# A drain of VectorE in place of the semaphore wait, where one Sinkhorn chain runs alone

## What is computed

```python
        def sinkhorn_log(logits, num_iters=SINKHORN_ITERS, tau=SINKHORN_TAU):
            Z = logits / tau
            ...
            def step(carry, _):
                u, v = carry
                u = -jax.nn.logsumexp(Z + v[..., None, :], axis=-1)
                v = -jax.nn.logsumexp(Z + u[..., :, None], axis=-2)
                return ((u, v), None)
            (u, v), _ = jax.lax.scan(step, (u0, v0), None, length=num_iters)
            return jnp.exp(Z + u[..., :, None] + v[..., None, :])
        ...
        H_res = sinkhorn_log(H_res_logits)
        H_pre = jax.nn.softmax(H_pre_logits, axis=-1)
        H_post = jax.nn.softmax(H_post_logits, axis=-1)
        g = jax.nn.sigmoid(gate)[0]
        I = jnp.eye(n, dtype=H_res.dtype)
        H_res = (1.0 - g) * I + g * H_res
        ...
        x_pre = jnp.einsum('btnc,btn->btc', x_streams, H_pre)
        y = x_pre @ W_branch
        x_mixed = jnp.einsum('btij,btjc->btic', H_res, x_streams)
        y_distributed = jnp.einsum('btc,btn->btnc', y, H_post)
        return (x_mixed + y_distributed).reshape(B, T, nC)
```

## Time and profile before

| | us |
|---|---|
| median of 3 runs (1103.5 to 1104.36) | 1104.23 |
| the profiled execution's own time | 1103.76 |
| its span | 1102.0 |
| PE busy | 1072.5 (97%) |
| DVE busy | 813.6 (74%) |
| ACT busy | 485.3 (44%) |
| POOL busy | 201.1 (18%) |

### The profile page before, as it was taken

One profiled execution on the slowest core, in us unless ns is written; L12 is line 12 of the kernel. 1 busy time (PEld: TensorE's weight loads), 2 busy tenths in 40 slices (PEclk: granted clock), 3 DMA queues, 4 the chain that ended last, 5 costly groups with the idle time before them and its releaser, 6 DMA issues.

```text
span 1102.0 us, 17847 instructions
## 1 busy us (share of the span) xinstructions
PE 1072.5 (97%) x6394; PEld 900.0 (82%) x6394; DVE 813.6 (74%) x1942; ACT 485.3 (44%) x1040; POOL 201.1 (18%) x199
## 2 busy tenths in 40 slices
PE   7999999999999999999999999999999999999578
PEld 6888888788888888888888888888888878888457
DVE  6887668667667878776667877757546798758998
ACT  4544434444444446544444455434313434342417
POOL 3000000223223233332332321000001032140001
PEclk9999999999999999999999999999999999999899
DMA  9975775255553333245445312699934705000001
GB/s 235 184 197 132 160 161 139 54 110 110 113 101 84 76 77 71 60 92 113 95 110 114 77 34 59 124 214 243 209 68 105 122 21 79 2 15 1 1 1 77
DMA packets 184830, 111.29 MB, mean 101 GB/s; under 512 B 108072, under 2 KB 174504, under 8 KB 184768
## 3 DMA queue, kind: packets, MB, share of 16 engines
q1 hardware_dynamic: 183136, 109.17, 46.2%
q10 hardware_dynamic: 1632, 1.31, 0.4%
HBM read 90.98 MB, written 18.94 MB: 100 GB/s over the span
## 4 chain that ended last, share of the span: by engine, by line
PE 90%; DVE 8%; DMA 1%; ACT 1%; issue 0%; ACTq 0%; DVEq 0%
PE ps L693 32%; PE ps L660 14%; PE ps L534 14%; PE ps L1041 8%; PE ps L523 4%; PE ps L721 4%; PE ps L704 4%; PE ps L1029 2%; PE ps L559 2%; PE ps L804 2%; DMA raw<-in_L_xattn_q_proj_w 1%; DVE small L2234 1%; DVE small L2238 1%; DVE small L2226 1%; DVE small L2230 1%; DVE small L2222 1%
## 5 line engine op out<-in xcount | busy, mean ns | idle before, releaser
L693 PE MATMUL ps<-wt,act 128*128 128x512 f32 x1536 | 381.1, 394 | 0.0
L693 PEld LDWEIGHTS ps<-wt,act 128*128 128x128 f32 x1536 | 278.1, 188 | 51.9 <-issue 0.4
L660 PE MATMUL ps<-act,wt 128*128 128x512 f32 x672 | 153.7, 390 | 0.0
L534 PE MATMUL ps<-wt,act 128*128 128x512 f32 x672 | 153.1, 389 | 0.0
L1171 ACT ACTIVATE wt<-raw 128x512 fp32r<-128x512 f32 x192 | 106.7, 625 | 93.2 <-PE ps L534 51.8
L534 PEld LDWEIGHTS ps<-wt,act 128*128 128x128 f32 x672 | 125.9, 188 | 26.0
L660 PEld LDWEIGHTS ps<-act,wt 128*128 128x128 f32 x672 | 125.8, 188 | 26.0
L1637 DVE STREAM_TRANSPOSE raw<-raw 128x1024 f32<-128x1024 f32 x92 | 107.9, 1217 | 22.1 <-DMA raw<-in_L_xattn_o_proj_w 21.2
L1041 PE MATMUL ps<-wt,act 128*128 128x512 f32 x480 | 121.4, 400 | 0.0
L1645 DVE TENSOR_TENSOR wt<-raw,wt 128x512 fp32r<-128x512 f32 x168 | 105.0, 682 | 16.4 <-ACT wt L1171 16.3
L2472 POOL TENSOR_TENSOR small<-small 128x4 f32<-128x4 f32 (+2 forms) x64 | 69.3, 1085 | 241.6 <-DVE small L1659 197.2
(11 more groups left out here) (188 smaller groups left out, 1324.7 us busy)
## 6 DMA issues: line engine op xcount, KB each, us to landing
xr<-in_ctx SPq DMA_DIRECT2D x64, 256.0 KB, 4.8
raw<-in_L_xattn_o_proj_w SPq DMA_DIRECT2D x32, 512.0 KB, 14.6
raw<-in_L_xattn_q_proj_w SPq DMA_DIRECT2D x28, 512.0 KB, 9.5
xr<-q_rows SPq DMA_DIRECT2D x16, 512.0 KB, 4.2
ot_hi<-spare SPq DMA_DIRECT2D x64, 128.0 KB, 2.0
act<-ot_hi SPq DMA_DIRECT2D x32, 256.0 KB, 10.2
q_rows<-G SPq DMA_DIRECT2D x28, 256.0 KB, 3.0
raw<-in_L_xattn_k_proj_w SPq DMA_DIRECT2D x8, 512.0 KB, 6.5
```

The costliest lines, as they stand in the source:

```text
L534: mm = pe.matmul(banks[t], lhs(p == 2, c, t), wt[:, n_slot, int(p == 1), c, :], start=(acc_from and q == 0), stop=(acc_to and q == 3 * NC ...
L660: mm = pe.matmul(acc[h], wt[:, par, int(p == 1), c, h * P:(h + 1) * P], act[:, 0, int(p == 2), c * UW:(c + 1) * UW], start=(q == 0), stop= ...
L693: mm = pe.matmul(bank, src[int(p == 2)][:, c, kt * P:(kt + 1) * P], wt[:, slot, int(p == 1), c, :], start=(q == 0), stop=(q == 3 * NC - 1))
```

## The change

`iterate` tells its steps when one chain is alone and nothing stands beside it. Then each of the six steps is preceded by `v.drain()`, an instruction of its own that holds VectorE's queue until the engine has finished what was issued, in place of the wait for `sk_step[c]`. The steps raise the semaphore as before. No instruction changes its place on any engine. That holds for five iterations of chain 0 at its beginning and for five of chain 2 at its end: 60 waits go and 60 drains come (VectorE's program has 2007 instructions in place of 1947). Fold steps and all iterations with two chains or with work beside keep the semaphore.

```diff
@@ -2155,6 +2155,12 @@
+            def settled(c, alone):
+                if alone:
+                    v.drain()
+                else:
+                    stepped(c)
+
...
-            def scale_cols(c):
-                stepped(c)
+            def scale_cols(c, alone=False):
+                settled(c, alone)
                 step(c, v.tensor_tensor(rows4(of(tk, c)), rows4(of(Kx, c)), over_i(ub[c]), ALU.mult))
 
-            def sum_rows(c, y):
-                stepped(c)
+            def sum_rows(c, y, alone=False):
+                settled(c, alone)
                 step(c, v.tensor_reduce(ua[c], rows3(of(y, c)), AX, ALU.add))
...
             def iterate(chains, beside=None):
 
+                alone = len(chains) == 1 and beside is None
                 fold = [c for c in chains if iterated[c] == folds[c]]
                 for c in chains:
                     iterated[c] += 1
                     if c in fold:
                         fold_outer(c)
                     else:
-                        scale_cols(c)
+                        scale_cols(c, alone)
...
                 for c in chains:
-                    sum_rows(c, Kx if c in fold else tk)
+                    sum_rows(c, Kx if c in fold else tk, alone)
...
                 for c in chains:
-                    invert_cols(c)
+                    invert_cols(c, alone)
```

More of the change, by code:

```diff
@@ L2214, in centre_cols, with invert_rows, scale_rows, sum_cols @@
                 step(c, v.reciprocal(ua[c], ua[c]))
-            def scale_cols(c):
-                stepped(c)
+            def scale_cols(c, alone=False):
+                settled(c, alone)
                 step(c, v.tensor_tensor(rows4(of(tk, c)), rows4(of(Kx, c)), over_i(ub[c]), ALU.mult))
-            def sum_rows(c, y):
-                stepped(c)
+            def sum_rows(c, y, alone=False):
+                settled(c, alone)
                 step(c, v.tensor_reduce(ua[c], rows3(of(y, c)), AX, ALU.add))
-            def invert_rows(c):
-                stepped(c)
+            def invert_rows(c, alone=False):
+                settled(c, alone)
                 step(c, v.reciprocal(ua[c], ua[c]))
-            def scale_rows(c):
-                stepped(c)
+            def scale_rows(c, alone=False):
+                settled(c, alone)
                 step(c, v.tensor_tensor(rows3(of(tk, c)), rows3(of(Kx, c)), over_j(ua[c]), ALU.mult))
-            def sum_cols(c):
-                stepped(c)
+            def sum_cols(c, alone=False):
+                settled(c, alone)
                 step(c, v.tensor_reduce(two(ub[c]), cols4(of(tk, c)), AX, ALU.add))
-            def invert_cols(c):
-                stepped(c)
+            def invert_cols(c, alone=False):
+                settled(c, alone)
                 step(c, v.reciprocal(ub[c], ub[c]))
@@ L2282, in iterate @@
                 for c in chains:
-                    invert_rows(c)
+                    invert_rows(c, alone)
                 if beside:
@@ L2286, in iterate @@
                 for c in chains:
-                    scale_rows(c)
+                    scale_rows(c, alone)
                 if beside:
@@ L2290, in iterate @@
                 for c in chains:
-                    sum_cols(c)
+                    sum_cols(c, alone)
                 if beside:
```

## The result

| | us |
|---|---|
| before, median of 9 runs (1103.15 to 1105.07) | 1104.09 |
| with the drains, median of 9 runs (1106.31 to 1109.41) | 1107.08 |
| ratio, with its 95% interval | 1.003 [1.0021, 1.0038] |
| the profiled execution's own time, and its span | 1109.41, 1107.6 |

The change makes the kernel 3.0 us slower, by the interval between 2.3 and 4.2. The forecast was 1107.0.

A forecast was written before the change was run, and what follows sets the result against it. PE, busy 97%, was taken as the bound, VectorE's steps mattering only where PE waits. Terms 0.76 + 0.84 + 1.14 = 2.74 us on 1104.23 gave 1107.0 us, range 1103.9 to 1110.0.

The forecast's parts named there:

- The bound and the seams: VectorE's steps matter only where PE waits: chain 0's lone iterations before 1019 us; chain 2's lie beside PE's last 23.62 us.
- x: Change in cost per lone step with a drain: taken as +0.07 us, bounded by -0.035 and +0.115.
- chain 0, first 18 steps: Three lone iterations before 1004.45 us: 1.26 us later, less 0.50 idle at line 2088, leaving 0.76 us.
- chain 0, next 12 steps: 1006.72 to 1009.49 us: 12 x 0.07 = 0.84 us, no idle time behind them, all reaching PE.
- chain 2, 30 steps: Kernel's end, 1087.45 to 1093.78 us: 2.10 us later, less 0.96 slack at the store, leaving 1.14 us.
- the slack is 0.96 us: At the last stores: SyncE's lands near 1100.56, ScalarE's near 1101.52 us, so 0.96 us of chain 2's delay is covered.
- tile 3's *first* diagonal: Ready at 1094.84 us, needed by PE near 1096.5: 1.6 us of slack, 0.5 us late after the change.
- SyncE's store would end the kernel: Sign at the kernel's end: POOL and SyncE's last store end the kernel instead of ScalarE's.
- costs no more than the wait: Rival at the lone steps: x between -0.035 and 0.03, time 1104.1 to 1104.6 us; chance 0.12.
- waits for the empty pipe either way: Rival at every lone step: a flush between operations sets the spacing, x = 0, time stays 1104.2 us; chance 0.10.
- Heavier: Rival at the lone steps: drain handshake makes x 0.09 to 0.15; 1109.7 us at 0.115, 1111.8 at 0.15; chance 0.16.
- The clock: Rival: TensorE's granted clock falls at PE's longer wait; 1.7 us seemed too little for that; chance 0.02.

The follow-up runs named there:

- first_only: Against the kernel before: drains only before chain 0's 30 lone steps, chain 2's keep the semaphore; 1106.34 us against 1103.74, ratio 1.0023.
- last_only: Against the kernel before: drains only before chain 2's 30 lone steps; 1104.88 us against 1103.74, ratio 1.0015.
- own_wait: Against the changed kernel: each drain replaced by a separate wait for the same semaphore, the step keeping its own; 1107.23 us against 1103.74 before, ratio 1.0034.
- two_drains: Against the changed kernel: two drains in place of one before each of the 60 lone steps; 1112.16 us against 1103.74 before, ratio 1.0083.
- late_attached: Kernel before, line 2260's last-ending wait put inside the step, the other ahead; doubled wait before chains 1 and 2's loop removed; 1103.55 us against 1103.68, ratio 0.9998.
- last_three: Against the kernel before: drains only before the 18 steps of chain 2's last three iterations; one profiled execution, 1104.38 us.
- pad18_before: Kernel before plus eighteen drains on VectorE ahead of add_last(1, 1), where it waits for PE; one profiled execution, 1106.46 us.
- drain_no_raise: Changed kernel, but chain 2's lone steps, except the last of each iteration, no longer raise the semaphore; one profiled execution, 1108.74 us.
- edges_away: Changed kernel plus 84 drains on VectorE where it waits for PE (60 before add_last(1, 1), 24 before logits(1)); one profiled execution, 1105.75 us.

## Why the prediction was right

**The bound and the seams** held. Lone steps cost where PE waits for DVE (chain 0's start) and where tile 3 is last (chain 2's end); first_only and last_only show each by itself.

**The price of a step**: x was taken as 0.07 from steps behind a separate wait and measured 0.057, inside the bounds of -0.035 and 0.115. That the next step is taken up only behind an instruction of its own is what own_wait, two_drains and late_attached show from different sides: it starts 0.044 us behind the end of the drain or the separate wait, and 0.044 of the 0.057 are this. That a step which has its wait inside meanwhile stands decoded and ready was my reading of the earlier trace rows and is not shown; what the runs show is that it starts 0.035 us behind the end of the step before. That a flush between two operations sets the spacing whatever stands there, by which nothing would change, was no more than a possibility. No run shows such a flush, and for these short dependent steps the spacing did depend on what stands between (0.211 us against 0.268).

**The terms of the sum**, in us:

| term | predicted | measured | why |
|---|---|---|---|
| chain 0, first 18 steps | 0.76 | 0.45 | x smaller; the idle time went, and was 0.59 |
| chain 0, next 12 steps | 0.84 | 1.20 | 0.63 for 11 steps, 0.17 for the wait on other work, about 0.4 for the late instruction 1244 |
| sum at line 2088 | 1.60 | 1.65 | 1.77 at PE's last run |
| chain 2, 30 steps | 1.14 | 1.19 | 0.8 through diagonals and PE, 0.4 through the stores |
| in all | 2.74 | 2.96 | medians 2.99 apart |

The measured values of the first two rows are the differences between the additions of line 2088 (4.24, 10.03 and 19.69 us behind the first step; 3.88, 9.58 and 18.04 before). The idle time at line 2088 is 0.59 us and not 0.50, since the addition doesn't need the step before it and can start 0.10 behind that step's start (1007.44 and 1007.54 us in the changed kernel, 1003.76 and 1004.45 before): 18 x 0.057 - 0.59 = 0.44.

So the total is better than its parts, and that it came within 0.3 us is luck. The smaller x alone would have given 0.53 + 0.68 + 0.75 = 1.96 us, which is under what can be told from no change. What I did not foresee made it up. First, I wrote that the twelve steps have "no idle time behind them" and counted twelve times x; I overlooked that the drain here waits for all that was issued before it, also for work that the step doesn't need (0.17 us at line 2224 behind `add_second`), and that the longer program has another instruction at 1244. Second, for chain 2 I wrote "the nearer edge is the store" and "the slack is 0.96 us". That edge is soft, as last_three shows. And the slack at PE was mis-sized: I held tile 3's *first* diagonal against PE's need, 1.6 us. But ScalarE writes a diagonal every 0.306 us, and PE's 128-wide matmuls use one every 0.22, so the later ones come closer; the fifth, ready near 1096.06 us, is wanted near 1097.35, which leaves some 1.3 us (estimate, from PE's 0.219 us an instruction and the diagonals' 0.306). By this a delay of 1.72 us would make PE's run some 0.4 us longer; it was 0.8, and the rest is not explained.

**What was to be seen**: 0.289 and 0.268 us in place of 0.30 and 0.28; the 0.50 us before line 2088 gone; PE waiting 1.75 us for "near 1.7"; PE's last run at 82.36 behind the first step, where 80.59 + 1.60 = 82.2 were forecast (in the profile's own time it is 1079.87 and not 1077.1, since that execution reached the chains 2.6 us late). Wrong was that SyncE's store would end the kernel; ScalarE's still does.

**The rivals**: "costs no more than the wait" and "waits for the empty pipe either way" fall with the 0.057. "Heavier" falls with own_wait. The clock did not fall at PE's longer wait: it is 1.00 in every window of 2 us from 1016 to 1026 us, and the block of twelve instructions behind it takes 3.01 us in PE's timeline and took 2.97 before. No run shows what a fall at that place would cost.

## What to carry to other kernels

The drain was not a cheap fence here: it is one more instruction through the engine's queue, it added 0.057 us to each lone step, and the step behind it started 0.044 us after it had ended. Of the three waits tried between these short dependent steps the one inside the waiting instruction was the shortest: 0.035 us from the end of a step to the start of the next, where it was 0.091 with a drain and 0.103 with a separate wait. Where a step had two waits, having the one that ends last inside and the other ahead was worth 0.07 us each time (late_attached). When a step off the critical path is made later, look at what else waits behind it on the same engine, and at which transfers go out together at the end, not only at when its result is wanted. Slack measured from one event to the next was too large here: 1.6 us at PE by the first diagonal, some 1.3 by the fifth (estimate above), since ScalarE writes them 0.306 us apart; and 0.96 us at the store, where a delay of 1.05 us already brought the end 0.57 us later (last_three).

## What the hardware showed that I had not expected

- Instructions at a few places in VectorE's program started 0.35 to 0.39 us late when a drain or a separate wait stood directly ahead. The places are 1116 (all twelve profiles), 1244 (seven), 1500 (pad18_before) and 2012 (two_drains), 128 or a multiple of it apart. In these 21 cases the instruction starts 0.39 to 0.43 us behind the end of that drain or wait, where 0.044 is usual. At the other places that lie a multiple of 128 behind 1116, 65 in the twelve profiles, the nearest drain or separate wait stands three instructions or more ahead, and at most 0.04 us of idle time show. In own_wait it is 0.41 us at 1244; the separate wait had ended while the four small operations of `add_second` still ran, so only 0.18 us of idle time show.
- That these are the edges of pieces of code is my reading. For it: in the changed kernel a queue for instructions, which carries 8192 bytes a packet, has one packet for every 120 to 129 records of VectorE from 1011 us on (and one besides, at 1067.75 us). This is the DMA view of 1010 to 1012 us (queue: packets, MB, share):

```profile
q14 instruction: 1, 0.01, 1.6%
```

  This packet is at 1011.03 us, behind the late step at 1010.37. So the step does not wait for that packet, and no run shows what it waits for. The kernel before has one between 1010 and 1012 us too, without a late step.
- The drain ended 0.018 us later behind a step that raises a semaphore than behind one that doesn't (0.047 us for 0.030 behind the step's end, drain_no_raise).
- A second drain, which finds the engine idle, added 0.05 us to a step (two_drains). The 24 in a row of edges_away started 0.04 us apart, but for the one at 1244.
- The first 995 us of this kernel vary by some 3 us from one profile to the next, as much as the whole effect, and the four long ones are those with a low granted clock of TensorE between 15 and 20 us (0.50 to 0.68, where the others have 0.93 to 1.00). In this kernel a difference of 2 to 3 us is better read from an event shortly before the change than from the span.
